# State-space scan in one core: block products taken from the full product, their mask put into the segment weights, and the out product reordered

## The reference

```
x = x + 0.5 * ffn(layernorm(x))
x = x + attn(layernorm(x))
x = x + 0.5 * ffn(layernorm(x))
```

```
state = state * dA_t[..., None, None] + einsum('bgcp,bgn->bgcpn', dtx_t, B_t)
y_t   = einsum('bgn,bgcpn->bgcp', C_t, state)
...
y = y + D * x
out = (y * rsqrt(mean(y*y) + EPS)) * norm_w * silu(z) @ out_proj_w
```

## Time and profile before

| what | value |
|---|---|
| median of 3 runs | 550.12 us (548.0 to 551.39) |
| profiled execution | 552.35 us |
| its span, first to last instruction | 550.6 us |
| granted TensorE clock, mean | 0.964 of full speed |
| scan, from XB of the first tile to the first FFN product | 253.3 to 440.6 us |

### The profile page before, as it was taken

How to read it: one execution, slowest core, us unless ns; L and a number is a source line. 1 busy time by engine, 2 the same in 40 slices (tenths; PEclk the granted TensorE clock), 3 DMA queues, 4 the chain that set the end, 5 groups by cost and what they waited for, 6 DMA issues and landing times.

```text
span 550.6 us, 17195 instructions
## 1 busy us (share of the span) xinstructions
PE 483.1 (88%) x7502; PEld 403.0 (73%) x7502; DVE 386.7 (70%) x734; ACT 280.1 (51%) x506; POOL 181.0 (33%) x229
## 2 busy tenths in 40 slices
PE   4999997989999889548899999999877699999997
PEld 3657886969887678436677778777766678898986
DVE  6998747474749996983687888777758747465542
ACT  3667624232438778766555665556635433232231
POOL 1100006084022221084566667665646311000000
PEclk9999998999999999778899999999989999999999
DMA  9940150000000000010000000000250000101011
GB/s 209 241 166 1 80 245 2 1 1 1 0 1 0 2 0 1 0 38 23 4 4 5 4 5 5 4 4 5 83 249 4 2 3 0 39 1 38 1 39 39
DMA packets 7163, 21.34 MB, mean 39 GB/s; under 512 B 688, under 2 KB 5296, under 8 KB 6448
## 3 DMA queue, kind: packets, MB, share of 16 engines
q1 hardware_dynamic: 6688, 18.08, 9.9%
q10 hardware_dynamic: 400, 2.16, 1.7%
HBM read 12.90 MB, written 6.55 MB: 35 GB/s over the span
## 4 chain that ended last, share of the span: by engine, by line
PE 35%; issue 9%; POOL 5%; DVE 2%; ACT 1%; POOLq 0%; DVEq 0%; ACTq 0%
PE intra L940 4%; POOL w L1169 3%; PE seg L819 3%; PE yo L68 2%; PE yo L70 2%; PE yo L69 2%; PE new L914 2%; PE XB L902 2%; PE XB L873 1%; PE seg L814 1%; PE prior L909 1%; PE intra L68 1%; PE intra L69 1%; PE intra L70 1%; PE yo L889 1%
## 5 line engine op out<-in xcount | busy, mean ns | idle before, releaser
L495 POOL TENSOR_TENSOR n_rstd<-n_ve,m_half 128x4 f32<-128x4 f32 x12 | 13.7, 1145 | 165.6 <-DVE n_ve L491 165.6
L1169 POOL TENSOR_TENSOR w<-xdt,ends 32x512 f32<-32x512 f32 (+3 forms) x63 | 66.5, 1074 | 1.7 <-PE prior L909 1.5
L959 ACT ACTIVATE seg<-seg 128x512 f32<-128x512 f32 x64 | 35.9, 579 | 52.7 <-PE seg L819 52.6
L597 DVE SCALAR_TENSOR_TENSOR cv<-pre,vec,cv 128x512 f32<-128x512 f32 x72 | 59.9, 846 | 3.8 <-ACT cv L653 2.1
L1038 DVE TENSOR_TENSOR mmat<-seg,gs 128x512 f32<-128x512 f32 x64 | 42.5, 684 | 11.8 <-ACT seg L959 11.5
L979 ACT ACTIVATE xbd<-xdt 32x512 f32<-32x512 f32 x64 | 39.9, 624 | 1.2
L819 PEld LDWEIGHTS seg<-abk,m_seg 96*32 96x32 bf16 x2048 | 21.2, 98 | 25.0 <-DVE mmat L1038 14.0
L940 PE MATMUL intra<-xbd,mmat 128*32 128x32 f32 x2048 | 34.3, 223 | 5.0 <-issue 5.0
L940 PEld LDWEIGHTS intra<-xbd,mmat 128*32 128x32 f32 x2048 | 32.0, 152 | 7.8 <-issue 6.0
L68 PE MATMUL pj<-n_xT,win 128*128 128x512 f32 x88 | 35.8, 407 | 1.1 <-PEq L118 1.1
L819 PE MATMUL seg<-abk,m_seg 96*32 96x64 bf16 x2048 | 28.4, 197 | 8.9 <-issue 5.7
(11 more groups left out here) (228 smaller groups left out, 1453.4 us busy)
## 6 DMA issues: line engine op xcount, KB each, us to landing
wgu_dram<-wgu SPq DMA_DIRECT2D x1, 2816.0 KB, 8.2
wgu<-wgu_dram SPq DMA_DIRECT2D x1, 2816.0 KB, 10.5
out<-x_res SPq DMA_DIRECT2D x4, 512.0 KB, 2.9
x_res<-in_x SPq DMA_DIRECT2D x1, 1536.0 KB, 24.4
wd_dram<-wd SPq DMA_DIRECT2D x1, 1536.0 KB, 11.5
wd<-wd_dram SPq DMA_DIRECT2D x1, 1536.0 KB, 13.7
gu_idx<-in_gu ACTq DMA_DIRECT2D x4, 352.0 KB, 8.1
gu_idx<-in_gu SPq DMA_DIRECT2D x4, 352.0 KB, 12.6
```

Source lines behind the costliest of these rows:

```text
L597: dve.scalar_tensor_tensor(dst, pre[:, x, k:k + GN].rearrange("p (t c) -> p t c", c=P), cw[:, x, k:k + 1], dst, ALU.mult, ALU.add).then_in ...
L959: act.activation(seg[u_ % 2][:, :, :], seg[u_ % 2][:, :, :], ACT.Exp).then_inc(s["exp_ok"], 1)
L1169: pool.tensor_tensor(heads(w[r, n, :]), heads(xdt[a % 2][r, :]), ends[a % 2][r, n * HEADS:(n + 1) * HEADS].unsqueeze(2) .broadcast_to([Q * ...
```

## The change

Six edits, one idea in two halves.

In the scan PE no longer computes the four diagonal blocks. ACT's copy into bg has 256 columns instead of 288, and four new copies of 32x32 take the blocks from the diagonal of the full product in BG straight to gs. They stand in ACT's order after exp of the ends and ahead of exp of unit 1; the next tile's B transpose on PE also waits for them.

POOL's product with `tri` goes. In its place m_seg and abk get a 97th row: -30000 in m_seg where the position lies before the token, and 1 in abk, so that exp gives 0 there. POOL fills both rows, the one of abk behind the blanks of w and xbd.

In the out product PE first adds the eight products of the high part of u, then waits for the low part and adds four, and only then does the two passes of ssum by ones.

```diff
-    m_seg, m_end, m_row, tri = T["m_seg"], T["m_end"], T["m_row"], T["tri"]
-    pool.memset(m_seg[:, :, :], 1.0).then_inc(built, 1)
+    m_seg, m_end, m_row = T["m_seg"], T["m_end"], T["m_row"]
+    K = PARTS * Q
+    pool.memset(m_seg[0:K, :, :], 1.0).then_inc(built, 1)
...
-    pool.memset(tri[:, :], 1.0).then_inc(built, 1)
+    pool.wait_ge(built, 3)
+    pool.memset(m_seg[K:K + 1, :, :], -30000.0).then_inc(built, 1)
...
-        pool.affine_select(out=tri[r, :], in_=tri[r, :], compare_op=ALU.is_ge, fill=0.0, base=0, pattern=[[1, Q]],
-                           channel_multiplier=-1).then_inc(built, 1)
...
+    pool.affine_select(out=m_seg[K:K + 1, :, :], in_=m_seg[K:K + 1, :, :], compare_op=ALU.is_gt, fill=0.0, base=0,
+                       pattern=[[-1, Q], [1, Q]], channel_multiplier=0).then_inc(built, 1)
...
+                    pool.wait_ge(T["blank"], 2)
+                    pool.memset(T["abk"][PARTS * Q:PARTS * Q + 1, :, :, :], 1.0).then_inc(T["blank"], 1)
+                    pool.wait_ge(T["blank"], 3)
...
-        bg = [sb(f"bg_{b}", [P, 2 * P + Q]) for b in range(2)]
+        bg = [sb(f"bg_{b}", [P, 2 * P]) for b in range(2)]
...
                     wait(pe, "bgs_ok", a)
+                    wait(pe, "gs_ok", NB * a)
                     pe.transpose(BG[:, 0:P], cv[:, a, 4, :], T["ident"][:, :])
-                    pe.matmul(BG[:, P:2 * P], cv[:, a, 4, :], cv[:, a, 5, :], start=True, stop=True)
-                    for b in range(NB):
-                        r = slice(Q * b, Q * b + Q)
-                        ins = pe.matmul(BG[r, 2 * P:2 * P + Q], cv[:, a, 4, r], cv[:, a, 5, r], start=True, stop=True)
-                    ins.then_inc(s["bg_ok"], 1)
+                    pe.matmul(BG[:, P:2 * P], cv[:, a, 4, :], cv[:, a, 5, :], start=True, stop=True
+                              ).then_inc(s["bg_ok"], 1)
...
                     wait(pe, "yf_ok", 4 * (z + 1))
-                    wait(pe, "red_ok", z + 1)
-                    pe.matmul(yo[:, HID:HID + 1], ssum[:, 0, :], T["ones"][:, 0:1], start=True, stop=True)
                     wait(pe, "uhi_ok", z + 1)
+                    for k in range(4):
+                        for hl in range(2):
+                            pe.matmul(yo[:, 0:HID], uh[:, 0, k, :], wout[:, hl, k, :], start=k + hl == 0, stop=False)
                     wait(pe, "ulo_ok", z + 1)
                     for k in range(4):
-                        ins = split_mm(pe, yo[:, 0:HID], uh[:, 0, k, :], uh[:, 1, k, :], wout[:, 0, k, :],
-                                       wout[:, 1, k, :], k == 0, k == 3)
-                    ins.then_inc(s["out_ok"], 1)
+                        pe.matmul(yo[:, 0:HID], uh[:, 1, k, :], wout[:, 0, k, :], start=False, stop=k == 3)
+                    wait(pe, "red_ok", z + 1)
+                    pe.matmul(yo[:, HID:HID + 1], ssum[:, 0, :], T["ones"][:, 0:1], start=True, stop=True
+                              ).then_inc(s["out_ok"], 1)
...
                     wait(act, "bg_ok", a + 1)
-                    wait(act, "gs_ok", a - 1)
                     wait(act, "new_ok", a - 1)
-                    act.activation(bg[a % 2][:, :], BG[:, 0:2 * P + Q], ACT.Copy).then_inc(s["bgs_ok"], 1)
+                    wait(act, "m_ok", (UNITS - 1) * (a - 1))
+                    act.activation(bg[a % 2][:, :], BG[:, 0:2 * P], ACT.Copy).then_inc(s["bgs_ok"], 1)
                     decays(a, 0)
+                    for b in range(NB):
+                        r = slice(Q * b, Q * b + Q)
+                        act.activation(gs[a % 2][r, :], BG[r, P + Q * b:P + Q * b + Q], ACT.Copy).then_inc(s["gs_ok"], 1)
                     decays(a, 1)
...
-                if do_a:
-                    wait(pool, "bgs_ok", a + 1)
-                    wait(pool, "m_ok", (UNITS - 1) * (a - 1))
-                    pool.tensor_tensor(gs[a % 2][:, :], bg[a % 2][:, 2 * P:], T["tri"][:, :], ALU.mult
-                                       ).then_inc(s["gs_ok"], 1)
...
-            ("m_half", [P, GT]), ("m_seg", [PARTS * Q, Q, Q], BF16), ("m_end", [P, NB + 1, P], BF16),
-            ("m_row", [P, 2, NB, Q], BF16), ("tri", [P, Q]), ("vec", [P, sum(n for _, n in VEC)]))
+            ("m_half", [P, GT]), ("m_seg", [PARTS * Q + 1, Q, Q], BF16), ("m_end", [P, NB + 1, P], BF16),
+            ("m_row", [P, 2, NB, Q], BF16), ("vec", [P, sum(n for _, n in VEC)]))
...
-                   ("ab", [P, PARTS, TILES, HEADS], BF16), ("abk", [PARTS * Q, NB, TILES, HEADS], BF16))
+                   ("ab", [P, PARTS, TILES, HEADS], BF16), ("abk", [PARTS * Q + 1, NB, TILES, HEADS], BF16))
```

More of the change, by code:

```diff
@@ L73, in build_masks @@
 def build_masks(pool, T, built):
-    m_seg, m_end, m_row, tri = T["m_seg"], T["m_end"], T["m_row"], T["tri"]
-    pool.memset(m_seg[:, :, :], 1.0).then_inc(built, 1)
+    m_seg, m_end, m_row = T["m_seg"], T["m_end"], T["m_row"]
+    K = PARTS * Q
+    pool.memset(m_seg[0:K, :, :], 1.0).then_inc(built, 1)
     pool.memset(m_end[:, :, :], 1.0).then_inc(built, 1)
     pool.memset(m_row[:, :, :, :], 1.0).then_inc(built, 1)
-    pool.memset(tri[:, :], 1.0).then_inc(built, 1)
+    pool.wait_ge(built, 3)
+    pool.memset(m_seg[K:K + 1, :, :], -30000.0).then_inc(built, 1)
     pool.wait_ge(built, 4)
     n = 4
-    for b in range(NB):
-        r = slice(Q * b, Q * b + Q)
[L86 to L93, removed]
-        pool.affine_select(out=tri[r, :], in_=tri[r, :], compare_op=ALU.is_ge, fill=0.0, base=0, pattern=[[1, Q]],
-                           channel_multiplier=-1).then_inc(built, 1)
-        pool.wait_ge(built, n + 1)
-        n += 1
+    for part in range(PARTS):
+        r = slice(Q * part, Q * part + Q)
+        pool.affine_select(out=m_seg[r, :, :], in_=m_seg[r, :, :], compare_op=ALU.is_gt, fill=0.0, base=0,
+                           pattern=[[0, Q], [-1, Q]], channel_multiplier=1).then_inc(built, 1)
+        pool.wait_ge(built, n + 1)
+        pool.affine_select(out=m_seg[r, :, :], in_=m_seg[r, :, :], compare_op=ALU.is_ge, fill=0.0, base=0,
+                           pattern=[[1, Q], [0, Q]], channel_multiplier=-1).then_inc(built, 1)
+        pool.wait_ge(built, n + 2)
+        n += 2
+    pool.affine_select(out=m_seg[K:K + 1, :, :], in_=m_seg[K:K + 1, :, :], compare_op=ALU.is_gt, fill=0.0, base=0,
+                       pattern=[[-1, Q], [1, Q]], channel_multiplier=0).then_inc(built, 1)
+    pool.wait_ge(built, n + 1)
+    n += 1
     ends = m_end[:, 0:NB, :]
@@ L555, in build_in_proj @@
         halves = [(k, slice(HEADS * k, HEADS * k + HEADS)) for k in range(2)]
-        MASKS = 4 + 2 * PARTS + NB + 4
+        MASKS = 4 + 2 * PARTS + 1 + 4
         CONVS = (4, 5, 0, 1, 2, 3)
@@ L833, in hidden @@
                     pe.wait_ge(loaded, 32)
-                    wait(pe, "bgs_ok", TILES)
+                    wait(pe, "gs_ok", NB * TILES)
                     wait(pe, "state_ok", TILES)
@@ L865, in product @@
                         last.then_inc(down_ok, 1)
-            pe.wait_ge(T["blank"], 2)
+            pe.wait_ge(T["blank"], 3)
             pe.wait_ge(T["abk_in"], 16 * PARTS * NB)
@@ L1099, in _ @@
                 if do_a:
-                    wait(dve, "gs_ok", a + 1)
+                    wait(dve, "gs_ok", NB * (a + 1))
                     wait(dve, "intra_ok", a - 1)
@@ L1174, in _ @@
             pool.wait_ge(s["set_ok"], 1)
-            pool.wait_ge(T["blank"], 2)
+            pool.wait_ge(T["blank"], 3)
             for a, b_, z, do_a, do_b, do_z in steps():
-                if do_a:
-                    wait(pool, "bgs_ok", a + 1)
-                    wait(pool, "m_ok", (UNITS - 1) * (a - 1))
-                    pool.tensor_tensor(gs[a % 2][:, :], bg[a % 2][:, 2 * P:], T["tri"][:, :], ALU.mult
-                                       ).then_inc(s["gs_ok"], 1)
                 if do_b and b_ < LAST:
```

## The result

The changed kernel takes 552.52 us (median of 20 runs, 549.54 to 554.26), the kernel before 549.85 (20 runs): ratio 1.0046, 95% interval 1.0029 to 1.0063. It is slower by 2.5 us, where 4.2 us less were forecast; its profiled execution took 552.85 (span 551.1).

The account below looks back on a forecast made before the run. The prediction took PE and the ACT-DVE chain, tied within 0.1 us in a scan step, to bound the kernel. Terms -2.8 + 0.3 - 1.7 = -4.2 us took the median 550.12 to 545.9, range 542 to 551.5.

Parts of the forecast that it names:

- Building masks and blanks: GpSimd's mask and blank steps before the scan: forecast to cost nothing, at most 3.8 us if their cover were gone.
- Block products: Scan, PE: dropping four 32x32 products makes what follows 0.20 us earlier; fourteen of sixteen steps gain, 2.8 us.
- Copies: Scan, ACT: each of four gs copies adds g = 0.12 us (bounds 0.07 and 0.26), hidden except in the first step.
- rival (a): Scan: ACT becomes the limit, each gs copy adding 0.26 us; 549.2 us, chance 0.16.
- Blocks and copies together: Scan: 2.8 us gained over fourteen steps, less 0.28 lost in the first step.
- The first step: First step of the scan: PE waits for mmat behind ACT, so the copies show; 0.28 us lost.
- Out product: Scan's out product, high parts first: PE waits less for the low part; 1.2 us in the last but one, 0.5 elsewhere.
- 97th row: Scan's segment sums on PE: one more row in 2048 pairs costs 0, bounds 0 and 8.0 us.
- rival (c): Scan, PE: the 97th row costs what intra's pairs cost, 8.0 us, so slower at 553.9 us; chance 0.08.
- Rival (b): Scan: PE's issue stalls, from instruction supply, swallow the block gain; 548.7 us, chance 0.14.
- Rival (d): Scan: stalls move and a 3.2 us stall in intra goes, a bigger gain; 542.7 us, chance 0.14.

Follow-up runs that it names:

- late_all: The changed kernel with GpSimd's three new steps (memset and select for m_seg's row, abk's ones row) moved just ahead of the scan; 0.9940 of the kernel before.
- before_new_out: The kernel before with only the out product reordered as in the change; 0.9921 of the kernel before, 4.3 us under it.
- late_ones: The changed kernel with only the ones row of abk moved behind GpSimd's last cast; 0.9979 of the kernel before.
- before_memset: The kernel before plus a GpSimd memset of one row of abk behind the blanks of w and xbd; 1.0108 of the kernel before, median 555.89 us.
- late_keep_blocks: late_all, but PE still computes the four diagonal blocks, which nobody reads; 1.0018 of the kernel before, 4.3 us above late_all.
- ones_mid: The changed kernel with abk's ones row set after the first group's second halo copy, beside VectorE's convolution taps; 0.9970 of the kernel before.

## Why the prediction was wrong

Wrong in sign, by one term. In ratios: out order -0.8% (-4.3 us); blocks, copies and masks, late_all over before_new_out, +0.2% (+1.0 us, the intervals allow -1 to +3); the place of GpSimd's new steps +1.07% (+5.9 us). They lead from one kernel to the next, so that they add up to the measured 2.5 proves nothing; each stands on its own runs. Without the failed term the change is late_all, 3.3 us faster, not far from the 4.2 forecast. That is luck in part: blocks and copies were forecast 3.5 us too good, the out product 2.6 too small.

- **Building masks and blanks, costed at nothing, at most 3.8 us: the step that failed.** The memset's length was right (3.8 by the earlier trace rows, 3.55 measured). I asked who waits for GpSimd's result, the halo copies, and not what its work holds up beside it. n_xn took 3.3 us more, PE stood and lost clock. The ones row alone cost 3.7 us by late_ones and 4.4 in the trace of before_memset; with the m_seg row, which held up f_hT, it was 5.9, more than the bound. The trace of before had the sign: four n_xn took 4.28 us beside the selects and 1.38 by themselves. Removing tri, taken as a relief, cost n_xn another 1.06.
- **Block products, 0.20 a step:** mis-sized, 0.29 (the end decays come 0.83 after a step's start instead of 1.12). I had counted the distance from the first of them to the end decays; what the other 0.09 is, no row shows.
- **Copies, g = 0.12:** mis-sized, 0.21, between my bounds and past the 0.17 at which, by my sum, the gain of a clean step is gone (2.63 less 1.96, in four). dt_tok's overlap of 0.13 doesn't hold for 32 columns: 184 ns long, 206 apart. The mechanism, ACT's chain tied with PE, was right: with 0.29 and 0.21 the same sum gives 1.48 + 0.39 + 0.84 + 3.09 = 5.80, as measured, halfway between the 5.53 forecast and the 6.09 of rival (a). By the Trainium skill's "ScalarE: Activation LUTs", section "What ACT_TABLE_LOAD costs", a copy was estimated to be 213 ns long and 120 apart from the next; the length is near, the distance isn't, and the measurement decides.
- **Blocks and copies together, -2.5:** two large terms that nearly cancel. From before_new_out to late_keep_blocks, on one chip, the copies, the row and the masks cost 4.9 us by the medians; from there to late_all the blocks give back 4.3. The sum, +1.0, doesn't settle the sign; the profiled executions of late_all and before_new_out, 545.34 and 548.54, point to a gain. This stays open for late_all; for the version with the copies on GpSimd it is a gain of 1.4 us. The first step lost 0.47 (4.98 to the second step's start in late_all, 4.51 before) where I had 0.28.
- **Out product, -1.7:** right in kind, measured -4.3. Missing were 0.1 in each step for the ssum passes (1.3 to 2.0 us), and the half clock behind the two waits (2.9 at the end instead of 1.2).
- **97th row, 0:** right. 32 pairs take 0.34 in late_all (296.06 to 296.40), 10.6 ns each; rival (c) fell.
- **Rival (b), stalls that swallow the gain:** issue stayed near 16 us, and the blocks were worth 4.3 us all the same (late_keep_blocks). Rival (d), the long stall in intra gone, didn't come either: it is 2.5 us in the changed kernel and 3.4 in late_all.

## What to carry to other kernels

A step on GpSimd isn't free because nobody waits for its result: ask what VectorE runs beside it, and put memsets and selects where VectorE has no one-input fp32 operation within SBUF, and selects also away from its operations with two inputs in SBUF. A tiny tile doesn't make such a step short; one partition of 4096 elements took 3.55 us. When two engines are tied, an edit that shifts work from one to the other may gain nothing, as between before_new_out and late_all; a third one that has time, here GpSimd for the gs copies, is where to try the work. And one trace of a kernel isn't its time: the same scan took 180.1 to 187.1 us in six.

## What the runs showed of the hardware

- A GpSimd memset of one partition holds up a VectorE operation with one fp32 input in SBUF for its whole length (3.68 us for one n_xn beside a memset of 3.55, after); VectorE's taps with two inputs run on beside it at 0.75 us (ones_mid).
- When GpSimd runs selects back to back, each such VectorE operation waits for one whole select: 1.33 us for one of 0.35 (late_all). An operation with two fp32 inputs in SBUF waits for a select too: 1.65 and 1.75 us instead of 0.69 (after).
- 32x32 copies on ScalarE out of PSUM stand 0.21 us apart and don't overlap (184 ns each), while 128x256 ones overlap by 0.13.
- Weight loads and products with 97 rows cost what those with 96 do: 10.6 ns a pair in late_all, 10.9 in the kernel before.
